# Reordering three places of a fused layer kernel: the opening, the entry of the value phase, the last head pair

## What is computed

```python
x = x + 0.5 * ffn(layernorm(x), A, B, Wr)
x = x + attention(layernorm(x), wq, wkv, wo)
x = x + 0.5 * ffn(layernorm(x), A, B, Wr)
# ffn: 64 experts of rank 16, the 16 best per token
scores = xf @ Wr.T; gates = softmax(top 16 of scores)
h = einsum('nd,krd->nkr', xf, A); out = einsum('nkr,kdr->nd', h * G, B) * 2
# attention: 4 sequences of 256 tokens, 32 heads of 128, causal
probs = softmax(q k^T * 192 ** -0.5); out = (probs v) @ wo
```

## Time and profile before

| | us |
|---|---|
| median of 3 runs | 1074.53 (1071.37 to 1075.76) |
| the profiled execution, its own time | 1073.46 |
| its span | 1071.5 |
| PE busy | 1048.3 (98%) |
| DVE / ACT / POOL busy | 693.1 / 481.9 / 511.2 |

### The profile page before, as it was taken

The page is one execution under the profiler, slowest core; times in us unless marked ns, Lnnn a source line. Parts: engine busy times, 40 slices in busy tenths (PEclk is TensorE's granted clock), DMA queues, the critical chain, the costliest instruction groups (busy, mean ns, idle before and its releaser), DMA issues.

```text
span 1071.5 us, 18633 instructions
## 1 busy us (share of the span) xinstructions
PE 1048.3 (98%) x5652; PEld 907.5 (85%) x5652; DVE 693.1 (65%) x1888; ACT 481.9 (45%) x1387; POOL 511.2 (48%) x443
## 2 busy tenths in 40 slices
PE   7999999999999999999999999999999999989998
PEld 7999778888778888888888888888888888869997
DVE  6778842433467777767677677676776776866552
ACT  4112355554365555545455555555455555521110
POOL 5331268995267547446365474474564652210000
PEclk8999999999999999999999999999999999999999
DMA  9700235672623213123122222131231221450000
GB/s 365 316 0 1 108 142 202 238 269 93 226 65 93 71 51 98 51 84 98 49 88 69 78 88 65 53 101 46 88 90 56 88 69 57 156 218 11 20 20 30
DMA packets 48910, 110.11 MB, mean 103 GB/s; under 512 B 5360, under 2 KB 21744, under 8 KB 47344
## 3 DMA queue, kind: packets, MB, share of 16 engines
q1 hardware_dynamic: 48880, 109.73, 29.7%
HBM read 73.79 MB, written 35.91 MB: 102 GB/s over the span
## 4 chain that ended last, share of the span: by engine, by line
PE 93%; DVE 4%; ACT 1%; issue 1%; POOL 1%; DMA 1%; SPq 0%; DVEq 0%; POOLq 0%; ACTq 0%
PE bank L227 27%; PE bank L229 27%; PE bank L228 27%; PE bank L423 4%; PE bank L413 3%; PE bank L441 2%; PE bank L268 1%; DMA upT_raw<-up_w 1%; PE bank L235 1%; PE bank L292 0%; DVE xn L754 0%; DVE prob L870 0%; DVE st L746 0%; DVE xc_lo L741 0%; DVE pT_lo L741 0%
## 5 line engine op out<-in xcount | busy, mean ns | idle before, releaser
L544 ACT ACTIVATE bank<-bank,nmax 128x128 f32<-128x128 f32 (+1 forms) x256 | 101.4, 397 | 92.7 <-DVE nmax L858 92.7
L1030 POOL TENSOR_TENSOR stage_w<-stage_w 128x256 f32<-128x256 f32 x128 | 91.6, 737 | 89.8 <-DMA stage_w<-wqk 87.3
L939 DVE TENSOR_TENSOR x<-bank,x 128x512 f32<-128x512 f32 x128 | 87.8, 687 | 41.0 <-PE bank L229 41.0
L858 DVE CUSTOM_DVE_ANT_0 bank<-bank,mask 128x128 f32<-128x128 f32 (+1 forms) x256 | 83.4, 387 | 35.9 <-PE bank L229 35.9
L227 PE MATMUL bank<-wo_lo,attT_hi 128*128 128x512 f32 x256 | 100.4, 392 | 1.3 <-POOL wo_lo L1014 1.3
L229 PE MATMUL bank<-wo_hi,attT_hi 128*128 128x512 f32 x256 | 100.2, 391 | 0.0
L228 PE MATMUL bank<-wo_hi,attT_lo 128*128 128x512 f32 x256 | 99.6, 389 | 0.0
L870 DVE TENSOR_SCALAR prob<-bank,rinv 128x128 f32<-128x128 f32 (+1 forms) x256 | 95.0, 413 | 4.5
L1012 POOL CAST wq_hi<-stage_w 128x256 fp32r<-128x256 f32 (+1 forms) x31 | 28.4, 916 | 145.1 <-PE bank L229 145.1
L227 PE MATMUL bank<-xc_lo,wq_hi 128*128 128x512 f32 x224 | 94.7, 423 | 0.7 <-ACT s7q L499 0.7
L227 PE MATMUL bank<-xc_lo,wk_hi 128*128 128x512 f32 x224 | 92.4, 412 | 1.8 <-DVE s7k L898 1.5
(11 more groups left out here) (144 smaller groups left out, 2979.5 us busy)
## 6 DMA issues: line engine op xcount, KB each, us to landing
stage_w<-wqk SPq DMA_DIRECT2D x32, 512.0 KB, 3.5
keep_v<-out_hl SPq DMA_DIRECT2D x64, 256.0 KB, 2.3
v<-keep_v SPq DMA_DIRECT2D x64, 256.0 KB, 2.8
stage_v<-wv SPq DMA_DIRECT2D x4, 2048.0 KB, 8.6
stage_wo<-wo SPq DMA_DIRECT2D x16, 512.0 KB, 3.3
keep_vraw<-out_raw SPq DMA_DIRECT2D x64, 128.0 KB, 2.1
v_raw<-keep_vraw SPq DMA_DIRECT2D x64, 128.0 KB, 3.1
upT_raw<-up_w SPq DMA_DIRECT2D x4, 544.0 KB, 6.5
```

What stands on the lines that cost most here:

```text
L544: nc.scalar.activation(sp[b][:, a:e], sp[b][:, a:e], ACT.Exp, bias=nmax[:, c:c + 1], scale=-1.0, accum_out=rsum[:, c:c + 1]).then_inc(s["e ...
L858: nc.vector.tensor_tensor_reduce(out=sp[b][:, a:e], in0=sp[b][:, a:e], in1=mask[:, a:e], scale=-SCALE, scalar=BIG, op0=ALU.add, op1=ALU.mi ...
L939: nc.vector.tensor_tensor(x[:, t, :], fp[t % 2][:, :], x[:, t, :], ALU.add).then_inc(s["fill_done"], 1)
L1030: nc.gpsimd.tensor_tensor(stage_w[:, out, :], stage_w[:, a, :], stage_w[:, b, :], op).then_inc(s["w_sum_s"], 1)
```

## The change

In the **opening**, tile 0's transposes wait no longer for the whole first slice of the up weight: slice 0 is split in two parts (384 and 704 columns), with tile 0's own split between them. Tile 1 gets its own transposed buffers (xT1_hi, xT1_lo) and the transposes of tile 1 move ahead of slice 3 of tile 0's product. Tile 1's up product is cut in three (pe_ffn_up_second): pieces 0 and 1 go to banks 7 and 3 right behind tile 0's product, ahead of the transposes of hg; piece 2 to bank 6 behind them. Tile 0's down product goes to bank 4 instead of 3, so tile 2's up product now waits for its sum (combined). POOL waits for tile 1's xn before it starts on the down weight. At the **entry of the value phase** tile 7's transposes move up by two columns of product 1, ACT takes tile 7's copies, weight 3 and tile 7's rounding earlier, DVE takes tile 7's combinations and their low part earlier, and POOL makes weight 2's low part in two halves, after comb_split 3, and weight 3's after DVE's last combination (comb_step), where it waited for comb_split 4. In the **last pair**, for j = 0 and 1 the second output tile moves behind the transposes of the probabilities, DVE does the next unit's maximum ahead of that tile's add, output tiles 2 and 3 of the last pair move ahead of the second FFN's first transposes, and DVE's normalise of that FFN's tile 0 moves behind the split of the last attended block.

```diff
@@ -148,6 +149,9 @@
+        xT1_hi = place("xT1_hi", [P, KD, P], F32R, at=where["s1"])
+        xT1_lo = place("xT1_lo", [P, KD, P], F32R, at=where["xa"])
@@ -184,6 +188,7 @@
         eb, tb, fb, ub, lb = bank[0:2], bank[2], bank[3], bank[4:7], bank[7]
+        ub2 = [lb, fb, ub[2]]
@@ -239,8 +244,13 @@
             for k in range(KD):
-                pe.wait_ge(s["up_split"], k + 1)
+                if k == KD - 1:
+                    pe_ffn_transpose(pe, 1)
                 for c, (a, b) in enumerate(CHUNKS):
+                    if c == 0:
+                        pe.wait_ge(s["up_split"], k + 1 if k == 0 else k + 2)
+                    elif k == 0 and c == 1:
+                        pe.wait_ge(s["up_split"], 2)
@@ -256,6 +266,17 @@
                 last.then_inc(s["up_ready"], 1)
+        def pe_ffn_up_second(pe, c):
+            pe.wait_ge(s["xT_split"], 2)
+            a, b = CHUNKS[c]
+            if c == 2:
+                pe.wait_ge(s["hg_ready"], 3)
+            for k in range(KD):
+                last = mm3(ub2[c][:, 0:b - a], xT1_hi[:, k, :], xT1_lo[:, k, :],
+                           upT_hi[:, k, a:b], upT_lo[:, k, a:b], k == 0, k == KD - 1)
+            last.then_inc(s["up_ready"], 1)
@@ -470,7 +491,7 @@
                     pe_output(pe, po, ta)
-                    if j < 2:
+                    if j < 2 and not final:
@@ -484,7 +505,7 @@
                         pe_m3(pe, "k", p + 1)
-                if out and j >= 2:
+                if out and (j >= 2 or final):
@@ -985,16 +1006,18 @@
                         dve_c12(dve, "k", p + 1)
-                if out and j >= 2:
+                if final and j < 3:
+                    dve_softmax_max(dve, u + 1)
+                if out and (j >= 2 or final):
...
                     dve_stats(dve, NT, 0, x[:, 0, :])
-                    dve_normalise(dve, NT, 0, x[:, 0, :])
-                else:
+                elif not final:
...
                 dve_attended(dve, p, 3)
+                dve_normalise(dve, NT, 0, x[:, 0, :])
@@ -1065,13 +1088,16 @@
-        def pool_v_weight(pool, n):
+        def pool_v_weight(pool, n, slices=1):
...
             r = ring[n % SLOTS]
-            nc.gpsimd.tensor_tensor(r[:, 1, :, :], stage_v[min(g, 1)][:, V_WEIGHT[i], :, :],
-                                    r[:, 0, :, :].bitcast(F32), ALU.subtract).then_inc(s["v_weight_split"], 1)
+            step = 2 // slices
+            for k in range(0, 2, step):
+                last = nc.gpsimd.tensor_tensor(r[:, 1, k:k + step, :], stage_v[min(g, 1)][:, V_WEIGHT[i], k:k + step, :],
+                                               r[:, 0, k:k + step, :].bitcast(F32), ALU.subtract)
+            last.then_inc(s["v_weight_split"], 1)
@@ -1108,9 +1134,13 @@
                 for j in range(VOPS):
-                    if VOPS * g + j == 1:
-                        pool.wait_ge(s["comb_split"], TH)
-                    if VOPS * g + j + 2 < VOPS * GROUPS:
+                    if VOPS * g + j == 0:
+                        pool.wait_ge(s["comb_split"], TH - 1)
+                        pool_v_weight(pool, 2, slices=2)
+                    elif VOPS * g + j == 1:
+                        pool.wait_ge(s["comb_step"], 6 * TH)
+                        pool_v_weight(pool, 3)
+                    elif VOPS * g + j + 2 < VOPS * GROUPS:
@@ -1286,12 +1316,13 @@
             pool_rstd(pool, 1, 0)
+            pool.wait_ge(s["xn_ready"], 2)
...
                                         ALU.subtract).then_inc(s["down_split"], 1)
-            pool.wait_ge(s["up_split"], KD)
+            pool.wait_ge(s["up_split"], KD + 1)
@@ -1344,14 +1375,15 @@
             pe_ffn_up_first(pe)
-            pe_ffn_transpose(pe, 1)
-
+            pe_ffn_up_second(pe, 0)
+            pe_ffn_up_second(pe, 1)
             pe_ffn_gated_transpose(pe, 0)
-            pe_ffn_up(pe, 1)
+            pe_ffn_up_second(pe, 2)
             pe_ffn_transpose(pe, 2)
-            pe_ffn_down(pe, 0, first=True)
+            pe_ffn_down(pe, 0, dst=ub[0], first=True)
...
             pe_ffn_gated_transpose(pe, 1)
+            pe.wait_ge(s["combined"], 1)
@@ -1375,10 +1407,10 @@
             pe_v(pe, 0, 0, 3)
+            pe_att_transpose(pe, NT - 1, dst=vyz[3])
...
             pe_v(pe, 0, 1, 1)
-            pe_att_transpose(pe, NT - 1, dst=vyz[3])
@@ -1412,9 +1444,11 @@
             pe_pair(pe, PAIRS - 1, final=True)
+            for t in (2, 3):
+                pe_output(pe, PAIRS - 1, t)
...
             pe.wait_ge(s["av_split"], 4 * PAIRS)
-            for t in range(2, NT):
+            for t in range(4, NT):
@@ -1435,15 +1469,19 @@
-            for k in range(KD):
+            act.wait_ge(up_loaded[0], 16)
+            for part in range(2):
+                a, b = FIRST[part]
+                act_copy(upT_hi[:, 0, a:b], upT_raw[:, 0, a:b]).then_inc(s["up_hi"], 1)
+                if part == 0:
+                    act_ffn_transposed(act, 0)
+            for k in range(1, KD):
...
                 act_copy(upT_hi[:, k, :], upT_raw[:, k, :]).then_inc(s["up_hi"], 1)
-                if k == 0:
-                    act_ffn_transposed(act, 0)
             act_down_hi(act, 0)
+            act_ffn_transposed(act, 1, xT1_hi)
...
             act_gate_exp(act, 0)
-            act_ffn_transposed(act, 1)
@@ -1475,11 +1513,11 @@
             act_v_snap(act, 0, 0, 3)
+            act_att_transposed_half1(act, NT - 1, src=vyz[3])
+            act_v_weight(act, 3)
             act_v_high(act, 0, 0, 0)
-            act_att_transposed_half1(act, NT - 1, src=vyz[3])
+            act_combined(act, NT - 1)
             act_v_high(act, 0, 0, 2)
-            act_combined(act, NT - 1)
-            act_v_weight(act, 3)
@@ -1518,17 +1556,24 @@
             dve_normalise(dve, 0, 0, x[:, 0, :])
-            for k in range(KD):
-                dve.wait_ge(s["up_hi"], k + 1)
+            for part, (a, b) in enumerate(FIRST):
+                dve.wait_ge(s["up_hi"], part + 1)
+                nc.vector.tensor_tensor(upT_lo[:, 0, a:b], upT_raw[:, 0, a:b], upT_hi[:, 0, a:b].bitcast(F32),
+                                        ALU.subtract).then_inc(s["up_split"], 1)
+                if part == 0:
+                    dve_ffn_transposed(dve, 0)
+            for k in range(1, KD):
+                dve.wait_ge(s["up_hi"], k + 2)
...
                                         ALU.subtract).then_inc(s["up_split"], 1)
-                if k == 0:
-                    dve_ffn_transposed(dve, 0)
...
                     dve_stats(dve, 1, 0, x[:, 1, :])
-
-            def step(t, n, att=True, last=False, early=False, stats=True, half1=False, combined=None):
+            dve_normalise(dve, 1, 0, x[:, 1, :])
+            dve_ffn_transposed(dve, 1, xT1_hi, xT1_lo)
+
+            def step(t, n, att=True, last=False, early=False, stats=True, half1=False, combined=None, opening=False,
+                     src=ub, down=fb):
@@ -1537,26 +1582,26 @@
                     dve_combined(dve, combined)
-                if not last:
+                if not last and not opening:
...
                     dve_normalise(dve, t - 2, 1, xt(t - 2))
-                dve_route(dve, n)
-                if not last:
+                dve_route(dve, n, src)
+                if not last and not opening:
...
                 if not early:
-                    dve_combine(dve, n - 1, t - 1)
+                    dve_combine(dve, n - 1, t - 1, down)
...
                 dve_stats(dve, t, 1, xt(t))
-            step(0, 0, att=False, early=True, stats=False)
+            step(0, 0, att=False, early=True, stats=False, opening=True)
             dve.wait_ge(s["xr_loaded"], 16)
-            step(1, 1, att=False)
+            step(1, 1, att=False, src=ub2, down=ub[0])
@@ -1577,13 +1622,13 @@
             dve_v_sum(dve, 0, 0, 0)
+            dve_att_transposed_half1(dve, NT - 1)
...
             dve_v_low(dve, 0, 0, 0)
-            dve_att_transposed_half1(dve, NT - 1)
+            dve_combined(dve, NT - 1)
...
             dve_v_low(dve, 0, 0, 2)
-            dve_combined(dve, NT - 1)
@@ -1606,8 +1651,10 @@
             dve_pair(dve, PAIRS - 1, final=True)
+            dve_output(dve, PAIRS - 1, 2)
+            dve_output(dve, PAIRS - 1, 3)
             dve_ffn_transposed(dve, NT)
-            for t in range(2, NT):
+            for t in range(4, NT):
```

More of the change, by code:

```diff
@@ L44 @@
 CHUNKS = ((0, 384), (384, 768), (768, UPW))
+FIRST = ((0, 384), (384, UPW))
 HEAD = (0, 1, 1, 0)
@@ L804, in dve_gated_transposed, with dve_route @@
                    hT_hi[:, 4 * i:4 * i + 4, :].rearrange("p k t -> p (k t)")).then_inc(s["hT_split"], 1)
[L806 removed]
+        def dve_route(dve, n, ub=ub):
             step = [5 * n]
@@ L1228, in _ @@
             load_wo(sync, 0)
-            sync.wait_ge(s["up_split"], KD)
+            sync.wait_ge(s["up_split"], KD + 1)
             for i, t in enumerate((upT_hi, upT_lo)):
```

5 lines of the change are left out of this document (2 added, 3 removed).

## The result

Forecast 1067.0 us. In the first measurement the changed kernel took **1065.42 us** (median of 5 runs, 1065.35 to 1066.97), the kernel before 1074.53 (1071.37 to 1076.41): ratio 0.9926, 95% interval 0.9908 to 0.9944. Six more runs, beside the last group of experiments, gave 1067.38 against 1074.80: 0.9934 (0.9920 to 0.9947). The eleven runs of the changed kernel fall into two groups with nothing between: three at 1065.4 (the lower group) and eight from 1066.9 to 1067.6 (the upper group); their median is 1066.97.

What follows compares the result with a forecast made beforehand. PE bounds the kernel, busy 1048.3 of 1071.5 us, so only its waits and low clock can be bought. Opening 1.7, entry 2.6 and last pair 2.7 sum to 7.0: 1066.5 or 1067.5, taken as 1067.0; range 1063.8 to 1070.6.

Steps and rivals of the forecast that it cites:

- the new wait: Opening: PE waits 2.4 us for tile 2's xn, whose root on POOL is queued behind all four down chunks.
- the rival: Opening: the clock falls in the wait for tile 2's xn, so the opening gives nothing; 1068.7 us, chance 0.24.
- both: Clock falls in the opening and DVE and POOL block each other at the entry; 1070.5 us, chance 0.08.
- xa's hold: Entry: xa takes 0.55 us, not held by POOL; if still held to 127.99, gain 0.8 instead of 2.6.
- the held combination: Entry: DVE's first of seven combinations waits for POOL's weight 2, until 130.1; an earlier one took 1.18 instead of 0.43.
- port rule: Entry: two-input DVE and SBUF-reading GpSimd instructions exclude each other; whichever issues first keeps the port for its whole length.
- The price: Entry: weight 3's new place delays DVE's low part until after 135.0, so PE waits 0.1 to 0.3 us.
- The rival of DVE and POOL in each other's way: Entry: each of seven combinations stands behind a POOL slice, comb_split 4 near 138; entry gain 0.8, 1068.8 us, chance 0.10.
- The two tiles: Last pair: two output tiles (2.8 us) fill the 2.01 us wait for the second FFN's first xn; gain 2.4.
- the 0.35 of the inner units: Last pair: units 0 and 1 gain at most 0.4 each, DVE's add costs three units 0.15 to 0.3; net 0.35.
- Slower by other loop addresses: Whole kernel: PE loses time at loop turns because loops sit at other addresses; 1081 at 0.6 us a turn, chance 0.03.

Runs made afterwards that it cites:

- E6: Changed kernel plus four needless 128x128 identity products ahead of tile 2's transposes in the opening, where PE waited 1.87 us; 1065.55 us.
- E1: Kernel before with only the opening's part of the change; 1073.26 us against 1074.86, ratio 0.9991.
- E2: Kernel before with only the part of the change at the entry of the value phase; 1070.57 us, ratio 0.9964.
- E11: Changed kernel with POOL's value-phase weight 2 neither kept back behind comb_split 3 nor cut in halves; 1069.55 us.
- E8: Changed kernel with POOL's weight 3 back at its old place, behind comb_split 4; 1065.76 us.
- E9: Changed kernel with the last pair's inner units in the old order, output tiles 2 and 3 still moved; 1067.63 us.
- E3: Kernel before with only the last pair's part of the change; 1070.48 us, ratio 0.9963.
- E7: Changed kernel with POOL's weight 2 not kept back behind comb_split 3 but still cut in halves; 1066.18 us.
- E12: The changed kernel run again without any edit, six runs; 1066.92 to 1067.56 us.
- E5: Changed kernel without POOL's new wait for tile 1's xn ahead of its down weight chunks; 1067.47 us.

## Why the forecast came out right

**The opening: mechanism right, the clock's chance wrong.** All starts up to the down product's were within 0.3 us of the forecast (hg's transposes at 21.15, forecast 20.95); the new wait is 1.87, not 2.4, since the work ahead of it ends at 24.0 and not at 23.5. Where the clock stays, tile 2's up product starts at 32.89 (E6), forecast 32.95, and the gain is 1.7 to 1.8 by the traces; where it falls, the gain is 0.25, and the rival said 0. I gave the rival 0.24, or 0.32 with "both". It held in eight of the changed kernel's eleven runs, going by their times; both traces of that kernel show it. The argument that failed is that a wait of 2.01 us in the last pair had not lowered the clock: that was one execution. In E1's trace it did not either, in E2's the same wait did. Nor did the new wait have to be longer than 2.01 us. One trace can show that a fall is possible, not that it is absent.

**The entry: 2.6 forecast, 2.75 measured.** The forecast's 137.7 for product 3 is in the old trace's times; 137.43 with the opening's 0.21 added back is 137.64. In the new trace it was to come 4.3 earlier and comes 2.85 earlier: what is missing there is the opening's part, lost to the clock. The parts were nearly so too: for xa's hold the bounds gave 1.8, E11 shows 1.76. That the held combination would hardly matter held (128.48, 1.29 us, off the path). The port rule of the Trainium skill (page "SBUF — State Buffer", section "Who interferes with whom") is borne out: DVE's low part, begun at 133.41 while POOL works (132.37 + 2.40), takes 2.45 us and ends 1.09 after POOL; with weight 3 behind it (E8) it takes 1.23. The price was forecast at 0.1 to 0.3 and is 0.15, net of the 0.1 that the other place costs (E8). The rival of DVE and POOL in each other's way did not come.

**The last pair: 2.7 forecast, 3.1 measured.** The two tiles gave 2.4, as worked out. The mis-sized term is the 0.35 of the inner units: 0.67, or 0.66 by E9. DVE's add does delay the division, by 0.12: the maximum before it ends at 929.23, the division's first step starts 0.47 later where it was 0.35 (933.52 against 933.17). ACT, then DVE; the last row is of before:

```profile
929.35 0.20 ACT L565 ACTIVATION_READ_ACCUMULATOR bank<-bank,nmax 128x1 f32 x1
...
929.09 0.69 DVE L960 TENSOR_TENSOR x<-bank,x 128x512 f32<-128x512 f32 x1
929.70 0.15 DVE L887 RECIPROCAL rinv<-rsum 128x2 f32<-128x2 f32 x1
...
933.52 0.17 DVE L866 RECIPROCAL rinv<-rsum 128x2 f32<-128x2 f32 x1 [0.35 <-ACT bank L544]
```

But the same move lets the maximum start ahead of the add, and the forecast charged the delay without this return. Unit 2, where the change is this order alone, shows the two cancel: 6.82 us to unit 3 (from 933.90), against 6.84.

**The sum.** 7.0 was forecast in the trace's terms; the trace of the upper group gives 6.1 and the 0.6 of the old execution, the lower group 7.6 and the 0.6. Against it stands what no term held: the kernel before loses 1.2 to 1.8 us more in its opening in some executions (E3, E2) and 1.5 in its last pair (E2), and its trace on record had neither. The change removes both waits. So the median moved by 7.4 to 9.1 us, more than the pair of traces explains. The same shows in the parts: the three alone moved their medians by 1.6, 4.3 and 4.4 us, 10.3 together, where their leads add up to 6.0. For the entry alone, which takes neither wait away, no run shows where its extra 1.5 us come from; of seven and eighteen runs it may be chance. Two omissions, the new fall and the old ones, worked against each other, so that the median of all eleven runs lies so near 1067.0 is in part luck. The first median fell 1.6 us below the forecast because three of its five runs were of the lower group; over all eleven runs it is 1066.97. All eleven lie in the range.

**Slower by other loop addresses** did not come: no loop is slower than in the old trace.

What stays open: why the fall comes in some executions only. Seven traces have this wait, of 1.87 to 1.92 us: five show the fall (the changed kernel twice, E1, E9, E11), two do not (E7 with 1.92, E8 with 1.91). In these two the early low stretch of the clock ended near 11.5 us, and so it did in E6; in the changed kernel's first trace, E1 and E9 it ended near 12.5, in E11 near 13.7, and E12 had none. That may be a sign, and is no more than that. Open, too, is how the median gain of the kernel before's own falls divides between its opening and its last pair.

## What to carry to other kernels

A wait of TensorE of about 2 us costs its length and, in some executions, some 1.5 us more in clock behind it: price it both ways, and look at several executions before saying that the clock holds. Then look for what releases it in the queue of another engine; here two small GpSimd instructions moved ahead of one wide one took 1.3 to 3.4 us off the whole. If a wide GpSimd instruction holds VectorE, cutting it in halves can already give most of what the cut and a wait in front of it give together, here 1.08 of 1.76 us.

## What the runs showed of the hardware

- The same wait lowered the granted clock in some executions and not in others: 2.01 us in the last pair (1.00 throughout in two traces, before and E1; 0.61, 0.50 and 0.58 in E2), 1.87 to 1.92 us in the opening (a fall in five traces of seven). It was worth about 1.5 us each time. With 1.01 us of idle time, after 1.05 us of needless products (E6), the trace shows no fall and none of the five runs lies in the upper group.
- The low stretch near the start moved in place as well: it began at 7.3 to 10.3 us and lasted 3 us or more in twelve traces, and was absent in two (E5, E12).
- A DVE instruction held by GpSimd gets in between two slices of the same GpSimd operation, though they follow each other at once: xa, begun at 123.62, ended at 125.10, where the slices took 2.68 us from 123.56 (E7). Behind one wide instruction, over at 127.90, it ended at 128.18 (E11).
- The same code of the head pairs ran at two paces, 0.1% or 0.6 us over 630 us apart: two of the fourteen traces at the slower (before, E3), twelve at the faster.
